# A decoder layer on one core: twelve layer norms whose last step is moved from VectorE to ScalarE

## The reference

```
x = x + mamba(layernorm(x))                       # 4 sequences x 512 rows x 256 columns
x = x + cross_attention(layernorm(x), context)    # 1601 context rows, a mask
x = x + routed_ffn(layernorm(x))                  # 8 experts, the best 2 of each row

layernorm(x) = (x - mean(x)) / sqrt(var(x) + 1e-5)   # over the 256 columns of a row
```

## Time and profile before

| | us |
|---|---|
| median of three runs | 1065.64 |
| the profiled execution, span | 1119.2 |
| PE busy | 908.4 (81%) |
| DVE busy | 670.0 (60%) |
| POOL busy | 599.3 (54%) |
| ACT busy | 446.0 (40%) |

### The profile page before, as it was taken

One profiled execution on the slowest core, in us unless ns is written; L12 is line 12 of the kernel. 1 busy time (PEld: TensorE's weight loads), 2 busy tenths in 40 slices (PEclk: granted clock), 3 DMA queues, 4 the chain that ended last, 5 costly groups with the idle time before them and its releaser, 6 DMA issues. The chain is left out here.

```text
span 1119.2 us, 16281 instructions
## 1 busy us (share of the span) xinstructions
PE 908.4 (81%) x5148; PEld 723.8 (65%) x5149; DVE 670.0 (60%) x1091; ACT 446.0 (40%) x827; POOL 599.3 (54%) x499
## 2 busy tenths in 40 slices
PE   5767667899969999788998779736279999999665
PEld 2344345576856677665677647735279999999564
DVE  5188789887789877876878433275034444443215
ACT  2555754467554476543555112231023333332111
POOL 2157785866666676658777132007743466425750
PEclk9989887999969999988999589957589999999686
DMA  9450020000170000530003100045513332212222
GB/s 321 157 199 1 2 113 38 1 15 1 40 264 1 16 1 2 199 103 7 9 1 110 42 7 8 20 155 191 146 39 115 115 115 75 78 37 70 61 89 90
DMA packets 48955, 85.45 MB, mean 76 GB/s; under 512 B 6292, under 2 KB 38696, under 8 KB 46856
## 3 DMA queue, kind: packets, MB, share of 16 engines
q1 hardware_dynamic: 43032, 65.77, 17.4%
q0 software_dynamic: 5872, 19.02, 5.6%
HBM read 65.64 MB, written 14.55 MB: 72 GB/s over the span
## 5 line engine op out<-in xcount | busy, mean ns | idle before, releaser
L413 POOL TENSOR_TENSOR u<-dtx,b_all 128x512 f32<-128x512 f32 x256 | 324.9, 1281 | 176.6 <-DVE h L662 172.9
L662 DVE TENSOR_TENSOR_SCAN h<-da,u 128x512 f32<-128x512 f32 x256 | 307.5, 1215 | 55.8 <-ACT da L497 33.9
L497 ACT ACTIVATE da<-dt_,a_neg 128x512 f32<-128x512 f32 x256 | 174.5, 690 | 105.9 <-DVE h L662 105.2
L785 PEld LDWEIGHTS ysum<-ident,h 128*128 128x128 f32 x1024 | 128.4, 152 | 94.5 <-DVE h L662 45.0
L785 PE MATMUL ysum<-ident,h 128*128 128x128 f32 x1024 | 157.7, 293 | 32.5 <-DVE h L662 25.5
L1421 DVE TENSOR_TENSOR hid<-act_,ps_u 128x352 f32<-128x352 f32 x78 | 40.4, 521 | 134.7 <-ACT act_ L1272 128.4
L965 PE MATMUL pv<-pT,ctx_n 128*128 128x128 f32 (+1 forms) x832 | 104.6, 276 | 1.4 <-DVE x_all L722 1.3
L965 PEld LDWEIGHTS pv<-pT,ctx_n 128*128 128x128 f32 (+1 forms) x832 | 98.4, 192 | 6.5 <-DVE x_all L722 3.2
L936 PE MATMUL pa<-ctx_t,xnT_a 128*128 128x401 f32 (+1 forms) x256 | 94.2, 502 | 3.6 <-ACT xnT_a L548 1.8
L1272 ACT ACTIVATE act_<-ps_g 128x352 f32<-128x352 f32 x78 | 36.1, 465 | 149.9 <-PE ps_u L1535 92.6
L1559 PE MATMUL ps_y<-w_hi,hidT_hi 128*128 x234 | 68.1, 291 | 19.0 <-issue 15.0
(11 more groups left out here) (217 smaller groups left out, 1796.4 us busy)
## 6 DMA issues: line engine op xcount, KB each, us to landing
b_all<-b_dram SPq DMA_DIRECT2D x16, 1024.0 KB, 4.7
ctx_t<-in_ctxT SPq DMA_DIRECT2D x4, 1601.0 KB
ctx_n<-in_ctx SPq DMA_DIRECT2D x4, 1536.0 KB
ffn_sorted<-yg SPq DMA_DIRECT2D x1, 4992.0 KB, 22.5
ffn_sorted<-y_sb SPq DMA_DIRECT2D x39, 128.0 KB
tok_in<-tok SPq DMA_DIRECT2D x35, 128.0 KB
mask<-in_mask SPq DMA_DIRECT2D x16, 200.1 KB, 2.4
w_raw<-in_w1T SPq DMA_DIRECT2D x4, 704.0 KB
```

Of the source, the lines that this page charges most:

```text
L413: nc.gpsimd.tensor_tensor(u[:, i % 2, :], dtx[:, j % 2, :], b_all[:, n, :], ALU.mult).then_inc(u_ok, 1)
L497: nc.scalar.activation(da[i % DS][:], dt_[:, j % 2, :], ACT.Exp, scale=a_neg[:, j, n:n + 1]).then_inc(da_ok, 1)
L662: nc.vector.tensor_tensor_scan(h[:, i % HS, :], da[i % DS][:], u[:, i % 2, :], 0.0, ALU.mult, ALU.add).then_inc(scan_ok, 1)
L785: last = nc.tensor.matmul(ysum[:, t * P:(t + 1) * P], h[:, i % HS, t * P:(t + 1) * P], ident[:], is_transpose=True, start=n == 0 and t == ...
```

## The change

It has three parts. First, the normalisation of each of the 48 tiles is an activation on ScalarE, Identity with a scale and a bias of their own for each row: r and `ln_shift` = -mean * r. Second, the Newton step is three fused instructions in place of four, `(var + eps) * r`, `(t * -0.5) * r`, `(t + 1.5) * r`, and two more instructions make the shift; VectorE therefore issues five small ones where it issued four, and no large one. Third, L252 goes: the epsilon is the bias operand of the logarithm, read from a tile `eps` that GpSimd fills once at the start, between two other fills. The statistics are unchanged. The tables get the steps of the new calls (`ln_m_apply`, `ln_a_apply`, `ln_f_apply`), and the copy of `ln_m` moves one or two steps.

```diff
+    "ln_a_norm": 8, "ln_a_turn": 8, "ln_a_apply": 9, "ln_a_copy": 10, ...          # STEADY
+    "ln_m_root": 2, "ln_m_norm": 1, "ln_m_turn": 1, "ln_m_apply": 3, "ln_m_copy": 4, ...
...
         def ln_statistics(dve, i, b):
...
                 nc.vector.bn_aggr(mv[:, t, :], stat[:, t, :]).then_inc(s["mv"], 1)
-            dve.wait_ge(s["mv"], b * T + T)
-            nc.vector.tensor_scalar(var[:], mv[:, :, 1], EPS, None, ALU.add).then_inc(s["var"], 1)
 
         def ln_root(act, i, b):
-            act.wait_ge(s["var"], b + 1)
-            nc.scalar.activation(log[:], var[:], ACT.Ln).then_inc(s["log"], 1)
+            if i == 0 and b == 0:
+                act.wait_ge(eps_ok, 1)
+            act.wait_ge(s["mv"], b * T + T)
+            nc.scalar.activation(log[:], mv[:, :, 1], ACT.Ln, bias=eps[:]).then_inc(s["log"], 1)
             act.wait_ge(s["log"], b + 1)
             nc.scalar.activation(r[:], log[:], ACT.Exp, scale=-0.5).then_inc(s["r0"], 1)
 
-        def ln_normalise(dve, i, b):
+        def ln_refine(dve, i, b):
             dve.wait_ge(s["r0"], b + 1)
-            nc.vector.tensor_tensor(tmp[:], r[:], r[:], ALU.mult).then_inc(s["newton"], 1)
-            dve.wait_ge(s["newton"], b * 4 + 1)
-            nc.vector.tensor_tensor(tmp[:], tmp[:], var[:], ALU.mult).then_inc(s["newton"], 1)
-            dve.wait_ge(s["newton"], b * 4 + 2)
-            nc.vector.tensor_scalar(tmp[:], tmp[:], -0.5, 1.5, ALU.mult, ALU.add).then_inc(s["newton"], 1)
-            dve.wait_ge(s["newton"], b * 4 + 3)
-            nc.vector.tensor_tensor(r[:], r[:], tmp[:], ALU.mult).then_inc(s["newton"], 1)
-            dve.wait_ge(s["newton"], b * 4 + 4)
+            nc.vector.scalar_tensor_tensor(tmp[:], mv[:, :, 1], EPS, r[:], ALU.add, ALU.mult).then_inc(s["newton"], 1)
+            dve.wait_ge(s["newton"], b * 5 + 1)
+            nc.vector.scalar_tensor_tensor(tmp[:], tmp[:], -0.5, r[:], ALU.mult, ALU.mult).then_inc(s["newton"], 1)
+            dve.wait_ge(s["newton"], b * 5 + 2)
+            nc.vector.scalar_tensor_tensor(r[:], tmp[:], 1.5, r[:], ALU.add, ALU.mult).then_inc(s["newton"], 1)
+            wait(dve, s["xn"], b * T)
+            nc.vector.tensor_scalar(shift[:], mv[:, :, 0], -1.0, None, ALU.mult).then_inc(s["newton"], 1)
+            dve.wait_ge(s["newton"], b * 5 + 4)
+            nc.vector.tensor_tensor(shift[:], shift[:], r[:], ALU.mult).then_inc(s["newton"], 1)
+
+        def ln_normalise(act, i, b):
+            act.wait_ge(s["newton"], b * 5 + 5)
             for t in range(T):
-                nc.vector.tensor_scalar(XN[i][:, t, :], rows(b, t), mv[:, t, 0:1], r[:, t:t + 1],
-                                        ALU.subtract, ALU.mult).then_inc(s["xn"], 1)
+                nc.scalar.activation(XN[i][:, t, :], rows(b, t), ACT.Identity, bias=shift[:, t:t + 1],
+                                     scale=r[:, t:t + 1]).then_inc(s["xn"], 1)
...
                 nc.gpsimd.memset(ones, 1.0).then_inc(ones_ok, 1)
+                nc.gpsimd.memset(eps[:], EPS).then_inc(eps_ok, 1)
                 nc.gpsimd.memset(zeros, 0.0).then_inc(zero_ok, 1)
...
+                            if i == when["ln_m_apply"]:
+                                if att_ and a:
+                                    act.wait_ge(pt_mm, a * NPT * T)
+                                ln_normalise(act, 0, m)
```

More of the change, by code:

```diff
@@ L78 @@
     "av_copy": (30, 41, 47, 54), "out": (31, 40, 47, 54), "x2": (32, 42, 47, 58), "ln_f_stat": 58, "ln_f_root": 60,
-    "ln_f_norm": 59, "ln_f_turn": 59, "ln_f_copy": 61, "router": (59, 60, 60, 60), "scores": 63, "ln_m_stat": 0,
-    "ln_m_root": 2, "ln_m_norm": 1, "ln_m_turn": 1, "ln_m_copy": 3, "in_proj": ((3, 3), (6, 7), (8, 9), (11, 12)),
+    "ln_f_norm": 59, "ln_f_turn": 59, "ln_f_apply": 61, "ln_f_copy": 61, "router": (59, 60, 60, 60), "scores": 63, "ln_m_stat": 0,
+    "ln_m_root": 2, "ln_m_norm": 1, "ln_m_turn": 1, "ln_m_apply": 3, "ln_m_copy": 4, "in_proj": ((3, 3), (6, 7), (8, 9), (11, 12)),
     "tap": (5, 10, 12, 14), "conv": (4, 10, 12, 14), "res_proj": ((19, 23), (24, 25), (28, 29), (30, 31)),
@@ L87 @@
     **STEADY,
-    "ln_m_root": 0, "ln_m_copy": 2, "in_proj": ((3, 3), (4, 4), (5, 5), (6, 6)), "tap": (5, 6, 7, 8),
+    "ln_m_root": 0, "ln_m_apply": 1, "ln_m_copy": 2, "in_proj": ((3, 3), (4, 4), (5, 5), (6, 6)), "tap": (5, 6, 7, 8),
     "conv": (6, 7, 8, 9), "res_proj": ((7, 7), (8, 8), (9, 9), (10, 10)), "res_copy": (9, 10, 11, 12), "silu": 14,
@@ L194, in mixer_phase @@
         attT = sb("attT", [P, KD, P])
-        ln_buf = [(sb(f"ln_stat{i}", [P, T, 6]), sb(f"ln_mv{i}", [P, T, 2]), sb(f"ln_var{i}", [P, T]),
-                   sb(f"ln_log{i}", [P, T]), sb(f"ln_r{i}", [P, T]), sb(f"ln_t{i}", [P, T])) for i in range(3)]
+        ln_buf = [(sb(f"ln_stat{i}", [P, T, 6]), sb(f"ln_mv{i}", [P, T, 2]), sb(f"ln_log{i}", [P, T]),
+                   sb(f"ln_r{i}", [P, T]), sb(f"ln_t{i}", [P, T]), sb(f"ln_shift{i}", [P, T])) for i in range(3)]
+        eps = sb("eps", [P, 1])
         wq, wk, wv, wo = (h[:, i, :].rearrange("p (k d) -> p k d", k=KD) for i in range(4))
@@ L244, in ln_statistics @@
         def ln_statistics(dve, i, b):
-            s, (stat, mv, var, log, r, tmp) = LN[i], ln_buf[i]
+            s, (stat, mv, log, r, tmp, shift) = LN[i], ln_buf[i]
             for t in range(T):
@@ L541, in body @@
                                 ln_root(act, 1, a)
+                            if i == when["ln_a_apply"]:
+                                wait(act, tok_st, 16 * T * a)
+                                ln_normalise(act, 1, a)
                             if i == when["ln_a_copy"]:
@@ L573, in body @@
                                 ln_root(act, 2, a)
+                            if i == when["ln_f_apply"]:
+                                act.wait_ge(LN[1]["tr"], a * KD + KD)
+                                ln_normalise(act, 2, a)
                             if i == when["ln_f_copy"]:
@@ L701, in body @@
                             if i == when["ln_a_norm"]:
-                                wait(dve, tok_st, 16 * T * a)
-                                ln_normalise(dve, 1, a)
+                                ln_refine(dve, 1, a)
                             if i == when["row_const"]:
```

22 lines of the change are left out of this document (10 added, 12 removed).

## The result

The changed kernel is slower: 1081.71 us median (1074.38 to 1084.02, 5 runs) against 1065.64 (1062.32 to 1070.9, 5 runs). The ratio is 1.0146, 95% interval [1.0117, 1.0174], so 12 to 19 us. The forecast was 1076.6. Five more timings of the same kernel gave 1082.54, ratio 1.0181 [1.0157, 1.0204].

What follows compares the result with a forecast made beforehand. TensorE sets the pace in long stretches; layer norms are chains of latencies, not VectorE load. Site delays 1.5 + 2.5 + 1.6 + 1.0 + 0.8 + 0.6 + 2.4 + 0.6 = +11.0 us on 1065.6 give 1076.6; 8-in-10 range 1060 to 1087.

Steps and rivals of the forecast that it cites:

- The operation's price: One ScalarE normalise takes 566 ns, four 2.01 us; the last tile comes 0.63 us later than from VectorE.
- The clear `ln_f` at the end: Last `ln_f`, no scan beside it, experts behind it: +0.6 us.
- The refinement and the epsilon: Layer norms' small instructions: 0.15 us more, dropped add saves up to 0.17; last tile 0.6 us later clear, 0.8 beside scans.
- The hold itself: Beside a scan, a small VectorE multiply waits for GpSimd's, 1.27 us against 1.26; fused instructions were assumed to wait too.
- Second `ln_m`: Layer norm at b = 0: normalisation stands behind `da` of step 3, which waits for a scan; +2.5 us.
- Start: First `ln_m`: the root waits for the fill of `eps`, then four slower tiles delay `in_proj`; +1.5 us.
- Third and fourth `ln_m`: Layer norms at b = 1, 2: later transposes delay `read_out`, convolution and output product by 0.8 us each; +1.6.
- The experts' phase is untouched: The phase behind the mixer was to take as long as before, adding nothing to the sum.
- third rival: ScalarE's queue costs more: `ln_a` beside scans 1.4 us each, instructions 690 ns, TensorE's clock +2; 1086 us, chance 0.15.
- VectorE's load (1055): Rival: VectorE's load decides near the layer norms, 11 sites gain 1.38 us each; 1055 us, chance 0.12.
- Only the first two `ln_m` cost: Rival: slack absorbs the other layer norms' delays; +4 us, 1069.6, chance 0.26.
- The free hold: Rival: fused instructions escape the wait for GpSimd, refinement beside scans ends 1.1 us sooner at five sites; 1071.1, chance 0.07.

Runs made afterwards that it cites:

- e3: The changed kernel with ScalarE's normalise as a plain copy, without scale and bias operands, so rows are not normalised; 1064.23 us, ratio 1.0.
- e1: The kernel before with only the fused refinement and the epsilon as bias tile, filled first on GpSimd; VectorE keeps the normalise; 1062.87 us, ratio 0.9989.
- e4: The changed kernel with the epsilon tile filled first on GpSimd and the second `ln_m` normalised right behind the root; 1075.06 us, ratio 1.0108.
- b_again: The kernel before, run again without edits for a profile near its median; 1064.67 us in that single execution.
- c_again: The changed kernel, run again without edits; 1082.54 us, ratio 1.0181.
- e8: The kernel before with 30 scrap operations on VectorE ahead of the first statistics; median 1081.5 us, ratio 1.0156.
- e2: The changed kernel with four scrap operations of 256 columns on VectorE behind the refinement of 11 layer norms; 1085.28 us, ratio 1.0199.
- e7: The kernel before with 15 scrap operations on VectorE ahead of the first statistics; median 1069.5 us, ratio 1.0043.
- e9: The changed kernel with 15 scrap operations on VectorE ahead of the first statistics; median 1089.3 us, ratio 1.0226.
- e5: e4 with the shift in one fused instruction, VectorE normalising tiles 0 to 2 and ScalarE tile 3; 1063.94 us, ratio 0.9998.

## Why the prediction was right, step by step

The forecast (1076.6, slower) was the case that came, and by the mechanism named: a chain of latencies in the mixer that ScalarE's longer instruction lengthens. The time was 5 to 6 us above it, so about a third of the loss is one that the prediction did not have.

- **The operation's price.** 566 ns expected, 588 measured; four in 2.01, measured 2.06 to 2.08. Right. e3 shows that this price, not the move of the work, makes the loss.
- **The clear `ln_f` at the end.** +0.6 expected. From the logarithm's start to the first tile's it was 1.34 and is 731.81 - 730.31 = 1.50; four tiles take 0.69 more. That is 0.85, less what the dropped add saved: +0.6 in the table. Right.
- **The refinement and the epsilon.** The sum at a clear site held, its parts did not: fusing saves more than I gave it (e1: 0.45 at an `ln_f` beside a scan), and the bias costs the logarithm 0.09, which I had left out. Beside a scan I expected 0.8; the three `ln_f` measured 0.5 each, 1.5 for 2.4. The step failed in taking every gain ahead of GpSimd's hold for swallowed: L268 averages 626 ns over twelve, so it is held at about five of them. In the first two `ln_f` (and the fourth `ln_m`) it is the first small instruction that is held, which I had not seen: L265, 1.09 us before, 0.73 in e1. What the prediction said of it, that an earlier start is swallowed, fails because the hold itself moves with the scan, and what stands behind the hold was never covered by it.
- **The hold itself.** It stays with fused instructions, 1.28 us beside GpSimd's 1.27. The Trainium skill (SBUF — State Buffer, "Who interferes with whom") has a VectorE instruction with two inputs in SBUF wait for a GpSimd one that reads SBUF; this trace agrees for fused ones.
- **Second `ln_m`**: +2.5 expected, 2.7 measured, the dearest site, by the mechanism named (`da` of step 3 ahead of it). **Start**: +1.5 expected, 1.3 measured, the wait for `eps` seen (5.7 us of L258's idle time), and e4 gives it back.
- **Third and fourth `ln_m`**: +1.6 expected, 0.2 + 1.35 measured. The sum is right, but single stretches move by as much: the third took 20.3 us in `b_again` and 18.7 in e1, at a granted clock of 0.73 and 0.78.
- **`ln_a`, b = 1, 2**: +0.5 each, measured 0.5 each. **b = 3**: +0.8 expected, 2.35 measured in c_again, but 0.4 in e4, where the granted clock in the same stretches was 0.74 and 1.00 for 0.66 and 0.91. The first profile of the changed kernel had 116.4 us there for before's 115.7, so 0.7. So some 2 us of c_again's stretch are clock, as in the experts. **Last `ln_a`**: 0.6 expected, 0.4 measured.
- **The mixer**: 742 for 731 expected, 741.75 for 730.1 measured. That it fits so closely is partly luck: the first pair of profiles has 739.6 for 730.7, 8.8 us. With b = 3 at its 0.7, the sites come to some 10 us for the 11.0: the three `ln_f` were put too high by 0.9, and the clock made up for it.
- **"The experts' phase is untouched"** is the step that failed. It took 338.9 us for 332.8. Of this about 1 us is a slower start, with the clock rising later (the first expert's `hid` is transposed 42.0 us behind the scores for 40.9). The two falls of the clock cost an estimated 3.5 (two stretches of 20 us at 0.91), and the two pairs of pauses that `b_again` doesn't have 3.4 (0.65, 1.02, 0.85 and 0.90). At 130 us behind the scores this kernel is 8.0 us behind, and 1.9 comes back after the last expert. The cause of the longer phase is not in the layer norms: the kernel before does the same when it starts 10 us late (e8). My third rival had "idle for longer, is granted less clock: +2", but put it in the mixer.
- **The rivals.** VectorE's load (1055) fell with e2. ScalarE's queue at 1.4 us per `ln_a` and 690 ns fell with the table. "Only the first two `ln_m` cost" fell too: 7.7 of the 11.7 us lie elsewhere. The free hold fell with L268. VectorE lost 19.8 us of work where I had said 15, and it counted for 3 at most.

What stays open is when the falls come. e4 and e7 end the mixer within 0.1 us of each other (733.8 and 733.9), and the experts take 339.1 and 332.6. The changed kernel itself once had 333.0, with its mixer ending at 739.6. And a pair of pauses of 2.5 us together left the clock at 2.4 GHz in e9, where one of 1.75 at 127 us behind the scores was followed by 1.2 GHz in c_again (matmuls of 0.50). So neither the moment nor the pauses' length decides alone. Nor is it shown why the waits for tokens 104 and 127 us behind the scores come with the first fall, only that `b_again`, e1, e3, e7 and the changed kernel's first profile, which lack that fall, lack these waits too (e5, also without it, has one at 123 us). The Trainium skill (TensorE: Matmul & The Clock Gate, "What's actually happening") says that what watches the array runs freely, without starting anew with a kernel. By that, equal pauses could come out differently; but the same falls in c_again, e2 and e4 are more regular than that suggests, and no run here separates it.

## What to carry to other kernels

Moving an operation to an idle engine pays only where the full engine's load is what the next wait ends on; in a chain of latencies the new engine's duration per instruction counts, once per site. Read the price of the operands too: two per-row operands made ScalarE's instruction 588 ns for 403, and without them the old time was back, though with values that are not normalised. At the start and the second `ln_m`, however, it was the place that cost (of `eps` among GpSimd's fills, of the normalise in ScalarE's order), and moving it earlier gave back all of 1.3 us and half of 2.7. And where a phase behind is sensitive to TensorE's clock, a forecast should leave it a range of its own, since being 8 to 12 us late mostly cost 6 to 7 us more there.
